# A convolution and quantized feed-forward kernel: x spans loaded with a shared block, two weight tiles and three spans handed to ScalarE, and the front of the kernel put in another order

## The reference, cut to what matters

```
def fake_quant(t, axis):
    s = max(abs(t), axis) / 127;  s = maximum(s, 1e-8)
    return clip(round(t / s), -128, 127) * s
def qlinear(x, w):
    return einsum('bsh,oh->bso', fake_quant(x, -1), fake_quant(w, 1))

y = conv1d(x, weight, taps=9, padding=4, groups=4)      # 32 channels, 8 of them in a group
y = y + (cond_128 @ c_weight.T)[:, :, None] + fside_S_0[None, :, None]
h = silu(qlinear(y, w_gate)) * qlinear(y, w_up)         # w_gate and w_up: 1376 x 512
out = x + qlinear(h, w_down)                            # w_down: 512 x 1376
```

## Time and profile before

| | |
|---|---|
| median of three runs | 283.59 us |
| the profiled execution | 283.23 us |
| its span in the trace | 281.4 us |
| PE busy | 273.0 us, 97% |
| DVE, ACT, POOL busy | 243.9, 196.3, 207.7 us |
| clock granted to PE | full in all 40 slices |

### The profile page before, as it was taken

How to read it: one execution, slowest core, us unless ns; L and a number is a source line. 1 busy time by engine, 2 the same in 40 slices (tenths; PEclk the granted TensorE clock), 3 DMA queues, 4 the chain that set the end, 5 groups by cost and what they waited for, 6 DMA issues and landing times.

```text
span 281.4 us, 5275 instructions
## 1 busy us (share of the span) xinstructions
PE 273.0 (97%) x1828; PEld 152.8 (54%) x1854; DVE 243.9 (87%) x412; ACT 196.3 (70%) x237; POOL 207.7 (74%) x215
## 2 busy tenths in 40 slices
PE   8989999999999999999999999999999999999995
PEld 5968754455554464644444744744444444444443
DVE  0998999999999989889888779789988889888973
ACT  2259999998778876666888836726787886666820
POOL 1478999998969787766888836846778888667732
PEclk9999999999999999999999999999999999999999
DMA  7999924597828998856589983424456764334265
GB/s 261 417 420 416 420 74 73 119 193 172 231 74 206 232 234 241 214 116 190 152 159 351 264 251 106 129 52 126 128 145 163 163 166 106 90 91 126 51 142 186
DMA packets 81577, 52.41 MB, mean 186 GB/s; under 512 B 69648, under 2 KB 70416, under 8 KB 81424
## 3 DMA queue, kind: packets, MB, share of 16 engines
q1 hardware_dynamic: 81120, 51.62, 67.3%
q10 hardware_dynamic: 432, 0.46, 0.5%
HBM read 26.77 MB, written 8.39 MB: 125 GB/s over the span
## 4 chain that ended last, share of the span: by engine, by line
PE 84%; DMA 6%; DVE 5%; SPq 3%; issue 2%; DVEq 0%
PE bank L1293 51%; PE bank L1317 26%; PE bank L1195 6%; DMA h_mem<-w_gate_up 6%; DVE gu_max L827 2%; DVE d_max L844 2%; SPq L332 1%; SPq L341 1%; PE bank L1332 1%; DVE sg_mem L899 1%; PE bank L1219 0%; DVE gu_scale L834 0%; SPq L335 0%; DVE sg_mem L978 0%; SPq L321 0%
## 5 line engine op out<-in xcount | busy, mean ns | idle before, releaser
L1293 PE MATMUL bank<-wgu_t,xq_mem 128*128 128x512 bf16 (+1 forms) x747 | 153.4, 356 | 1.1
L532 POOL TENSOR_TENSOR sg_mem<-sg_mem,gu_scale_row 128x512 f32<-128x512 f32 (+1 forms) x96 | 111.1, 1164 | 36.3 <-ACT sg_mem L691 36.3
L1293 PEld LDWEIGHTS bank<-wgu_t,xq_mem 128*128 128x128 bf16 x768 | 73.7, 98 | 73.2 <-DVE h_mem L912 1.6
L691 ACT ACTIVATE sg_mem<-sg_mem,x_scale 128x512 f32<-128x512 f32 (+1 forms) x96 | 62.7, 672 | 30.2 <-DVE sg_mem L899 29.8
L1317 PE MATMUL bank<-wd_t,hq_mem 128*128 128x512 bf16 (+1 forms) x336 | 77.8, 379 | 0.3
L912 DVE SCALAR_TENSOR_TENSOR h_mem<-bank,x_scale,sg_mem 128x512 f32<-128x512 f32 (+1 forms) x96 | 65.7, 691 | 9.0 <-POOL sg_mem L532 7.9
L899 DVE TENSOR_TENSOR sg_mem<-bank,gu_scale_row 128x512 f32<-128x512 f32 (+1 forms) x96 | 59.7, 626 | 9.4 <-PE bank L1293 9.2
L696 ACT ACTIVATE h_mem<-h_mem,h_inv 128x1376 f32<-128x1376 f32 (+1 forms) x32 | 45.3, 1419 | 28.4 <-DVE h_inv L820 28.4
L1317 PEld LDWEIGHTS bank<-wd_t,hq_mem 128*128 128x128 bf16 (+1 forms) x341 | 33.3, 98 | 39.7 <-issue 0.2
L917 DVE TENSOR_REDUCE h_max<-h_mem 128x1 f32<-128x1376 f32 x31 | 48.8, 1576 | 0.0
L704 ACT ACTIVATE hq_mem<-h_mem 128x1376 bf16<-128x1376 f32 (+1 forms) x32 | 42.0, 1315 | 0.2
(11 more groups left out here) (72 smaller groups left out, 174.0 us busy)
## 6 DMA issues: line engine op xcount, KB each, us to landing
xo_mem<-x SPq DMA_DIRECT2D x24, 256.0 KB, 3.1
out<-xo_mem SPq DMA_DIRECT2D x24, 256.0 KB, 2.2
slab<-x_pairs SPq DMA_DIRECT2D x8, 576.0 KB, 7.9
slab_taps<-x_pairs SPq DMA_DIRECT2D x7, 576.0 KB, 5.5
hq_mem<-w_gate_up SPq DMA_DIRECT2D x7, 512.0 KB, 11.3
slab_taps<-w_down SPq DMA_DIRECT2D x3, 688.0 KB, 14.8
h_mem<-w_gate_up SPq DMA_DIRECT2D x4, 512.0 KB, 15.9
slab_taps<-x SPq DMA_DIRECT2D x1, 2048.0 KB, 9.5
```

What stands on the lines that cost most here:

```text
L532: pool.tensor_tensor(s, s, gu_scale_row[:, 1, at:at + n], ALU.mult).then_inc(silu_scaled, 1)
L691: act.activation(s, s, ACT.Silu, scale=x_scale_of(i)).then_inc(silu_done, 1)
L1293: last = pe.matmul(bank[n % 2][:, 0:cols], xq_t[:, g, k, P * c:P * (c + 1)], wgu_t[:, m, k, at:at + cols], start=(k == 0), stop=(k == KT - 1))
```

## The change

The change leaves the loop and the end as they are, and does five things in the front.

1. The two spans of a pair are now the same part of the two halves of the 512 positions (positions 64i and 256 + 64i), and a slab holds 33 blocks, in which neighbouring pairs share one. Each pair that is not the first of its group brings eight blocks, 512 KB; the first brings nine. The weights' columns are put in the same order before the launch.
2. `BY_ACT` gains the spans 3, 6 and 7: ACT copies them and POOL adds the shift, where DVE did both.
3. ACT rounds the weight tiles 0 and 1, where POOL did.
4. The scales of the weight tiles are made by one instruction for two tiles, and those of `w_down` for three tiles and then one.
5. The lists of SP, POOL, ACT, DVE and PE are written anew up to tile 6. Among others: tile 1 of the weights is loaded ahead of pair 3; there are 12 matmuls on zeros, not 16; `turn_down_row` stands behind `gate_or_up(5, 1, 2)`, not behind `gate_or_up(1, 0, 0)`; pairs 8 and 9 are loaded one behind the other, after `turn_w_down(1)` and ahead of `turn_hq(0)` and `turn_w_down(2)`; two `fold_y` of group 1 (9 and 11) stand behind tile 5, later than before.

```
-        BY_ACT = [2, 4, 5] + list(range(8, 18)) + list(range(19, 32, 2))
+        BY_ACT = list(range(2, 18)) + list(range(19, 32, 2))
+        W_BY_ACT = [0, 1]
...
+        def new_words(k):
+            i = k % PAIRS
+            return slice(N * (NEW * i + (1 if i else 0)), N * (NEW * i + BLOCKS))
...
-                sp.dma_start(pair_blocks(k).rearrange("p b n -> p (b n)"), x_pairs[k, :, :]).then_inc(pair_in[k], 16)
+                words = new_words(k)
+                sp.dma_start(slab_words[g % 2][:, words], x_slabs[g, :, words]).then_inc(pair_in[k], 16)
...  (SP)
             load_w(0)
+            load_w(1)
             load_pair(3)
-            load_w(1)
+            load_pair(4)
             load_other_taps()
-            load_pair(4)
...
-            turn_w_down(0)
             turn_yq(5)
             turn_yq(6)
+            turn_w_down(0)
             turn_w_down(1)
+            load_pair(8)
+            load_pair(9)
+            turn_hq(0)
             turn_w_down(2)
-            load_pair(8)
-            turn_hq(0)
             turn_w_down(3)
...  (ACT)
+            def round_w(j):
+                r = rows(j)
+                act.wait_ge(gu_inv_ready, j + 1)
+                for m in range(2):
+                    wj = w_in[j % W_SLOTS][0:r, m, :]
+                    last = act.activation(wj, wj, ACT.Copy, bias=MAGIC + LOW, scale=gu_inv[0:r, j, m:m + 1])
+                last.then_inc(w_rounded_by_act, 1)
...
             copy_span(2)
+            copy_span(3)
             copy_span(4)
             copy_span(5)
+            round_w(0)
+            round_w(1)
+            copy_span(6)
+            copy_span(7)
             copy_span(8)
             copy_span(9)
             copy_gate_up(0)
             copy_gate_up(1)
             copy_xq(0)
-            copy_xq(1)
             round_y(0)
             round_y(1)
             round_y(2)
...  (DVE)
             def weights_scale(j, n):
-                for k in range(j, j + n):
-                    r = rows(k)
-                    dve.wait_ge(gu_max_ready, k + 1)
-                    dve.tensor_scalar(gu_scale_mem[0:r, k, :, 0:3], gu_max[0:r, k, :], 1.0 / QMAX, SMALLEST_SCALE,
-                                      ALU.mult, ALU.max).then_inc(gu_scale_ready, 1)
+                r, last = rows(j), 3 * (j + n) - (1 if n == 2 else 0)
+                dve.wait_ge(gu_max_ready, j + n)
+                dve.tensor_scalar(gu_scale_mem[0:r, 3 * j:last, 0:3], gu_max[0:r, 3 * j:last, :], 1.0 / QMAX,
+                                  SMALLEST_SCALE, ALU.mult, ALU.max).then_inc(gu_scale_ready, n)
...
             down_top(0)
             down_top(1)
-            down_scale(0)
+            scale_gate(0, 1)
             down_top(2)
-            scale_gate(0, 1)
             down_top(3)
-            down_scale(1)
-            down_scale(2)
-            down_scale(3)
             scale_gate(0, 2)
             scale_gate(1, 0)
-            down_inverse(0)
+            down_scales(0, 3)
             multiply_up(0, 0)
...  (PE)
-            run_empty(up_bank[1], 16)
+            run_empty(up_bank[1], 12)
             conv_pair(4)
             turn_gate_up(0)
             turn_gate_up(1)
             turn_xq(0)
-            turn_xq(1)
             conv_pair(5)
             turn_gate_up(2)
+            turn_xq(1)
+            turn_xq(2)
             turn_gate_up(3)
-            turn_xq(2)
             conv_pair(6)
...
             gate_or_up(0, 0, 2)
             gate_or_up(1, 0, 0)
-            turn_down_row()
+            gate_or_up(0, 1, 1)
             gate_or_up(1, 0, 1)
             gate_or_up(1, 0, 2)
             gate_or_up(0, 1, 2)
...
+            turn_down_row()
+            gate_or_up(6, 1, 0)
+            down(0)
             down(1)
```

More of the change, by code:

```diff
@@ L31, with adaln_ffn @@
 SECOND = 5
-def adaln_ffn(nc, x, x_first, x_pairs, cond_ctx_bias, taps, w_gate_up, w_down, out):
+def adaln_ffn(nc, x, x_first, x_slabs, cond_ctx_bias, taps, w_gate_up, w_down, out):
     N, C, L = x.shape
@@ L187, in conv_before @@
             return q - 2 if FRONT + 2 <= q < 3 * SPANS + 2 else q - 4
-        BY_ACT = [2, 4, 5] + list(range(8, 18)) + list(range(19, 32, 2))
+        BY_ACT = list(range(2, 18)) + list(range(19, 32, 2))
+        W_BY_ACT = [0, 1]
+        W_BY_POOL = [j for j in range(JT) if j not in W_BY_ACT]
         BY_DVE = [q for q in range(SLOTS) if q not in BY_ACT]
@@ L591, in _ @@
             scale_silu(3, 2)
+            convert_down(2)
             convert_down(3)
@@ L725, in _ @@
             copy_gate_up(5)
-            round_y(3)
-            round_y(4)
             copy_span(12)
             copy_span(13)
+            copy_xq(3)
+            copy_xq(4)
             copy_gate_up(6)
             copy_gate_up(7)
-            copy_xq(3)
-            copy_xq(4)
+            silu(0, 0)
             copy_gate_up(8)
@@ L736, in _ @@
             copy_gate_up(10)
-            silu(0, 0)
+            silu(0, 1)
             copy_xq(5)
             copy_xq(6)
-            silu(0, 1)
+            round_y(3)
+            round_y(4)
             round_y(5)
@@ L743, in _ @@
             silu(1, 0)
-            round_down(0)
-            round_down(1)
+            round_y(6)
             silu(1, 1)
@@ L776, in _ @@
             round_h(4)
-            silu(5, 2)
-            silu(6, 0)
-            silu(6, 1)
             convert_h(4)
-            silu(6, 2)
             round_h(5)
@@ L1082, in _ @@
             token_scale(3)
+            token_inverse(2)
             multiply_up(4, 0)
-            token_inverse(2)
+            multiply_up(4, 1)
+            scale_gate(6, 0)
             token_inverse(3)
-            fold_y(11)
-            multiply_up(4, 1)
             multiply_up(4, 2)
-            token_top(4)
-            token_scale(4)
-            scale_gate(6, 0)
             scale_gate(6, 1)
@@ L1459 @@
     ci = np.shape(L0_cond_weight)[1]
-    spans, pairs = length // 64, length // 128
-    blocks = 64 // STEP + 1
+    half, span = length // 2, 64
+    blocks = half // STEP + 1
     x_wide = np.zeros((n, c, length + 2 * PAD), np.asarray(x).dtype)
     x_wide[:, :, PAD:PAD + length] = x
-    x_pairs = np.stack([x_wide[:, :, 64 * i:64 * i + STEP * blocks] for i in range(spans)])
-    x_pairs = np.ascontiguousarray(x_pairs.reshape(pairs, 2, n, c // ci, ci, blocks, STEP).transpose(3, 0, 1, 4, 6, 5, 2)
-                                   .reshape(c // ci * pairs, 128, blocks * n))
+    x_slabs = np.stack([x_wide[:, :, half * i:half * i + STEP * blocks] for i in range(2)])
+    x_slabs = np.ascontiguousarray(x_slabs.reshape(2, n, c // ci, ci, blocks, STEP).transpose(2, 0, 3, 5, 4, 1)
+                                   .reshape(c // ci, 128, blocks * n))
     weight = np.asarray(L0_cond_weight).reshape(c // ci, ci, ci, 2 * PAD + 1).transpose(2, 0, 1, 3)
@@ L1472 @@
     taps = taps.reshape(128, c // ci, -1)
-    x_first = np.concatenate((taps[:, 0], x_pairs[0, :, 0:FIRST * n]), axis=1)
+    x_first = np.concatenate((taps[:, 0], x_slabs[0, :, 0:FIRST * n]), axis=1)
     w_gate_up = np.stack((np.asarray(L0_ffn_w_gate), np.asarray(L0_ffn_w_up)), axis=1)
+    w_gate_up = w_gate_up.reshape(-1, 2, 2, half // span, span).swapaxes(2, 3).reshape(-1, 2, length)
     arrays = {
```

231 lines of the change are left out of this document (120 added, 111 removed).

## The result

The changed kernel takes 286.8 us (median of 5 executions, 285.21 to 287.04) against 283.59 for the kernel before, measured beside it (283.51 to 284.24): a ratio of 1.0104 (95% interval 1.0086 to 1.0122). It is 3.2 us slower, outside the predicted range of 282.3 to 283.9. The profiled execution is the fastest of the five: it took 285.21 us with a span of 283.4 us at a granted clock of 1.0. The other four took 286.76 to 287.04 us, and their record shows a mean clock of 0.994.

What follows compares the result with a forecast made beforehand. The front was taken as bound by bytes, then by a chain of DVE. A 0.8 us gain less 0.1 us of stalls gave -0.7 us, a median of 282.9 us against 283.59; range 282.3 to 283.9.

Steps and rivals of the forecast that it cites:

- Bytes, minus 0.95 us: Front loads: 384 KB fewer before the w_down tiles, so w_down tile 1 lands at 33.05 instead of 34.0 us.
- Pair 3 late and covered: Front: PE waits 0.5 us for pair 3, but pair 4 starts at 14.85 instead of 14.88 us, so nothing is won.
- Rounding on ACT: Weight tiles 0 and 1: four roundings of 0.62 us, 2.5 us from 12.85, hidden in ACT's idle time.
- POOL's tiles 8 to 10: POOL rounds these weight tiles from 29.75 to 33.85 us; PE finishes its work before piece (1,0,1) at 38.1 us.
- the forecast wait of 0.7 us: PE, ready at 38.1 us, idles 0.7 us for scale_gate(0,2) before piece (1,0,1) at 38.8 us.
- DVE's chain up to `scale_gate(0,2)` at 38.8 us: DVE's work from w_down tile 1 on ends scale_gate(0,2) at 38.8 instead of 39.93 us; PE then starts (1,0,1).
- Less three or four small scale instructions of 0.07 us (0.2 us): DVE's chain in the front: it keeps its length less these instructions, saving 0.2 us.
- a stall of 0.5 us: Rival: PE gets ahead and DVE takes it back between 38.8 and 60 us; time 283.3 us, chance 0.20.
- 0.1 us of stalls from 38.8 us to the loop: PE's tightest pieces (4,0,0) and (5,0,0) find banks just in time; stalls taken as 0.1 us, between none and 0.5.
- Pair 8's load in time: Load issued at 55.5, landing at 60.7 us, just in time for PE; rival that it comes late, 284.7 us, chance 0.10.
- The clock: Rival: PE's clock falls to half around 12 to 17 us; time 285 us, chance 0.03.
- The forecast of a wait for DVE between 40 and 60 us: Sign of a wrong prediction: PE waits over 0.3 us for a DVE release between 40 and 60 us.

Runs made afterwards that it cites:

- x3: The kernel before with plain instead of transposing loads and only the change's first part, shared blocks and shorter loads: 282.4 us, ratio 0.9966.
- w1: The kernel before with its 66 transposing DMAs replaced by plain ones, the base for the variants: 283.61 us, ratio 1.0003.
- z2: The changed kernel with plain loads, scale_silu(0, 2) moved ahead of three conversions on GpSimd: 284.03 us in one execution, the kernel before 284.75 beside it.
- w3: The changed kernel with plain loads and three single 128x1 scale instructions for the grouped one: 282.69 us, ratio 0.997.
- x1: The changed kernel with plain loads, its grouped scale instruction made over nine padded columns instead of 128x3: 282.66 us, ratio 0.9974.
- z1: w3 with an unused 128x3 scale instruction behind its three single ones: 285.33 us in one execution, the added instruction 2.85 us.
- x2: The changed kernel with plain loads and 36 matmuls on zeros before gate_or_up(0, 1, 2): 285.08 us, ratio 1.0067.
- m3: Separate kernel copying x to out, six small DVE instruction shapes each beside five GpSimd products of 1.23 us: scale operations over two or three columns wait for one product.
- x4: Separate copy kernel, 128x3 beside twelve runs of six GpSimd instructions, varying kind, semaphores and a preceding DVE instruction: no wait beyond the GpSimd instruction in flight.
- y1: Separate copy kernel, GpSimd in the changed kernel's order, 128x3 arriving at twelve points of the run: no wait beyond the GpSimd instruction in flight.
- y2: The kernel before with plain loads and three unused DVE instructions per loop block from block 22: 128x3 waits at most one GpSimd instruction, 0.91 us.
- w4: The kernel before with plain loads, the scales of w_down tiles 1 to 3 made by one 128x3 instruction: 284.11 us, ratio 1.0012.
- w2: The changed kernel with plain loads in place of the transposing ones: 286.69 us, ratio 1.0097.

## Why the prediction was wrong, by its own steps

- *Bytes, minus 0.95 us.* Right. The three loads of `w_down` were issued from 18.45 for 1.38 us and took 14.2 us (median) to land: 33.1 us for tile 1 by the same sum as before, forecast 33.05. The 407 GB/s of the earlier trace rows are low for the stretch (421 from 20 to 34 us, by which 384 KB are 0.93 us); that changed nothing. x3 carries 0.64 us (against w1) to 0.86 us (against the kernel before) of it to PE.
- *Pair 3 late and covered.* Right: a wait of 0.61 us (0.5), pair 4 at 14.79 (14.85), with 0.24 us before it that waited for no load.
- *Rounding on ACT.* Right, and hidden: four in 2.56 us from 12.57 (2.5 from 12.85). ACT has one gap of 0.21 us between 17.02 and 35.03.
- *POOL's tiles 8 to 10.* Ended at 34.42, not 33.85. Not foreseen was a wait of 0.82 us for the weights' scales before the turn at 18.84; by it and the waits for POOL PE was ready for piece (1,0,1) at 36.31 + 2.49 = 38.80 (the twelve matmuls before it; 2.49 us is their time in z2), not 38.1, so the forecast wait of 0.7 us was 0.11. Neither cost anything, because the piece had to wait for `scale_gate(0,2)` in any case.
- *DVE's chain up to `scale_gate(0,2)` at 38.8 us.* Right: the pair of gates starts at 38.33, where the pair of the earlier trace rows starts at 39.49, 1.16 us earlier (forecast 1.15). The 0.44 us that I took for its duration is the distance to the next start; the first gate takes 0.52 us and ends at 38.85, and PE starts (1,0,1) at 38.90, not 38.8. The misreading cost the forecast 0.1 us.
- *"Less three or four small scale instructions of 0.07 us (0.2 us)".* This is the step that failed. I took grouped instructions for a saving by counting them, with the duration of single ones. One of them, `down_scales(0, 3)`, costs 3.02 us where three took 0.27: w3, x1 and z1 show it from both sides. I looked at DVE's own row for the price and never at what POOL did beside it; and I looked for stalls in PE's banks, where a stall of 0.5 us was my worst case. The 0.1 us of stalls in the sum measured 2.55 us.
- *0.1 us of stalls from 38.8 us to the loop.* Right without that instruction: in x1 PE runs 24.58 us without a listed wait and reaches pair 8 at 60.81 (forecast 60.75). With it PE stands for 2.55 us.
- *Pair 8's load in time.* Right where it was put to the test: in x1 the load is issued at 55.91 and no wait shows. In z2, issued at 57.84, it made PE wait 0.76 us before 62.44, so this rival was close.
- *The clock.* I gave it a chance of 0.03, at 12 to 17 us. A mean clock of 0.994 came in four of the five executions, and x2 supports the new wait as its cause; where it fell is not shown. No profiled run bears out the rule on transposes that I cited from the Trainium skill: the clock's row of the page shows full speed in the slices of the turns, before and after.

The sum: the profiled execution is 1.98 us slower (285.21 against 283.23), and the rest of the 3.2 us lies in the medians: the changed kernel's stands 1.6 us over its profiled execution, with the clock at 0.994, and that of before 0.36 us over its own: 1.98 + 1.6 - 0.36 = 3.2. Take the instruction away and -0.9 us is measured (w3: 282.69 against 283.61 for w1), where I had -0.7. x3 has as large a gain without the new order, which fits the walk: 0.95 of the 1.15 us by which it had DVE's chain earlier were bytes. The forecast of a wait for DVE between 40 and 60 us as the sign of a wrong prediction was met.

Open is the size in the kernel. The wait ends with the GpSimd instruction in flight in m3, x4, y1, y2 and w4, and over four of them in the changed kernel, w2, x2 and z1, always at the same place. It is bound to the place and not to the buffers (z1); kind, order and semaphores of GpSimd's instructions by themselves don't make it (x4, y1). One difference that no run settles is the length of GpSimd's run: at that place its list shows no wait from 26.68 us on, and in m3, x4 and y1 its runs were of some 7 us at most. w4 had a run as long (from 28.31 us) but met its last instruction. What the other engines and the transfers do at that place was not varied either. So it is shown that this form beside a working GpSimd makes the loss, and not why it waits for four instructions.

## What to carry to other kernels

Before grouping small VectorE instructions, see what GpSimd does at that moment and keep a scale operation out of the form "same small count in source and destination, both in SBUF" (counts of two and three were measured; one column passes); a padded layout took 0.15 us and was held up in no run. Price a merged instruction from a row of its own form, or bound it from above by the neighbour's run, even where it handles three numbers. When a change has several parts, ask first which resource the front is bound by: here the part that saved bytes was worth all of the gain of about 1 us, and the grouping of three small instructions cost 4.0 us (w2 less w3, by their medians; 2.2 us between their profiled executions at full clock).

## What was unexpected of the hardware

- A VectorE scale operation over 128x2 or 128x3 in SBUF waits for GpSimd: 1.21 us in m3 where 128x9 takes 0.16 us; 3.02 us in the kernel. The trace books the wait as busy time and names no releaser.
- The wait spans four GpSimd instructions at one place (3.02, 3.02, 3.02 and 2.85 us) and one at most wherever else another followed (m3, all 24 cases of x4 and y1, one of y2).
- A PE wait of 2.55 us at 40.5 us went with a mean clock of 0.994 and some 1.6 us more (once 3.4) in 7 of 10 executions; with 36 matmuls on zeros in it, in none of 5. The place of the fall was not seen.
